# Memory of lines: two multiplications for the next tile, the decay of the state on ScalarE, and tails ahead of the last memory

## The reference, cut to what matters

```python
w1 = (x_prev @ w1w.T).reshape(B, T, H, 4);  w2 = (x @ w2w.T).reshape(B, T, H, 4)
write_lines = exterior(w1, w2)            # 6 differences of products, divided by their norm
r1 = (x @ r1w.T).reshape(B, T, H, 4);       r2 = (x @ r2w.T).reshape(B, T, H, 4)
read_lines = exterior(r1, r2)
Jw = jnp.einsum('bthi,ij->bhtj', write_lines, _J6)
outer = Jw[..., :, None] * Jw[..., None, :]              # 6 x 6 per token and head
# M[t] = sum over s < t of decay ** (t - s) * outer[s]
rd_M = jnp.einsum('bhti,bhtij->bhtj', rd, M_all)
score_M, score_M2 = jnp.sum(rd_M * rd, axis=-1), jnp.sum(rd_M * rd_M, axis=-1)
mem_score = (1 - alpha) * score_M + alpha * score_M2
```

## Time and profile before

| | |
|---|---|
| median of 3 runs | 1919.88 us (1919.46 to 1920.75) |
| the profiled execution | 1922.61 us |
| its span in the profile | 1920.7 us |
| TensorE busy, share of the span | 1856.6 us, 97% |
| VectorE | 1603.5 us, 83% |
| ScalarE | 1491.9 us, 78% |
| GpSimd | 929.2 us, 48% |

### The profile page before, as it was taken

The page is one execution under the profiler, slowest core; times in us unless marked ns, Lnnn a source line. Parts: engine busy times, 40 slices in busy tenths (PEclk is TensorE's granted clock), DMA queues, the critical chain, the costliest instruction groups (busy, mean ns, idle before and its releaser), DMA issues. The chain is left out here.

```text
span 1920.7 us, 61287 instructions
## 1 busy us (share of the span) xinstructions
PE 1856.6 (97%) x22646; PEld 1108.6 (58%) x22646; DVE 1603.5 (83%) x5443; ACT 1491.9 (78%) x4110; POOL 929.2 (48%) x568
## 2 busy tenths in 40 slices
PE   7999999999999989999999999889999999999999
PEld 3777774577775443344444448637777635777754
DVE  5899974899995668999999949979999658999945
ACT  4999995699998362777777763469999847999973
POOL 2788861488883050000000036648888405888820
PEclk9999999999999995999999999999999999999999
DMA  6212230122221041111111000002121201222211
GB/s 179 50 44 50 45 70 6 29 47 48 47 54 42 1 151 38 42 41 41 42 41 41 26 7 5 2 20 51 44 51 44 62 6 36 45 50 45 67 23 44
DMA packets 76330, 85.33 MB, mean 44 GB/s; under 512 B 17327, under 2 KB 50803, under 8 KB 75907
## 3 DMA queue, kind: packets, MB, share of 16 engines
q1 hardware_dynamic: 75839, 81.40, 17.0%
q10 hardware_dynamic: 196, 0.02, 0.0%
HBM read 20.83 MB, written 8.39 MB: 15 GB/s over the span
## 5 line engine op out<-in xcount | busy, mean ns | idle before, releaser
L336 ACT ACTIVATE probs<-probs,negmax 128x128 f32<-128x128 f32 x1024 | 401.9, 402 | 2.3 <-DVE negmax L411 1.9
L2328 ACT ACTIVATE gprobs<-ps_global 128x1024 f32<-128x1024 f32 (+3 forms) x384 | 291.5, 811 | 126.2 <-PE ps_global L1765 103.5
L291 POOL TENSOR_TENSOR rot<-rot 128x1024 f32<-128x1024 f32 x128 | 302.5, 2363 | 143.9 <-DVE rot L381 143.9
L297 POOL TENSOR_TENSOR qk<-rot,cnorm 128x1024 f32<-128x1024 f32 x128 | 244.0, 1906 | 173.6 <-issue 150.9
L304 POOL TENSOR_TENSOR probs<-probs,iden 128x1024 f32<-128x1024 f32 x128 | 243.0, 1898 | 47.2 <-DVE iden L419 46.5
L2010 DVE TENSOR_REDUCE maxes<-ps_global 128x1 f32<-128x512 f32 (+2 forms) x384 | 222.1, 639 | 11.6 <-PE ps_global L1728 6.5
L411 DVE CUSTOM_DVE_ANT_0 probs<-ps_attn,masks 128x128 f32<-128x128 f32 x1024 | 226.2, 287 | 0.8 <-issue 0.8
L336 ACT ACTIVATION_READ_ACCUMULATOR probs<-probs,negmax 128x1 f32 x1024 | 204.2, 199 | 0.0
L1723 PE MATMUL ps_global<-kq 48*128 48x512 bf16 (+3 forms) x768 | 197.3, 346 | 7.1 <-DVE maxes L2010 1.8
L2240 POOL CAST m_parts<-m_turn 32x128 bf16<-32x128 f32 x16 | 4.5, 282 | 364.7 <-DVE m_turn L2024 364.7
L377 DVE TENSOR_TENSOR rot<-ps_attn,rotary 128x512 f32<-128x512 f32 x256 | 175.1, 684 | 1.8 <-PE ps_attn L202 1.5
(11 more groups left out here) (235 smaller groups left out, 4501.5 us busy)
## 6 DMA issues: line engine op xcount, KB each, us to landing
v_first<-v_second SPq DMA_DIRECT2D x256, 128.0 KB, 2.3
hs<-z_a SPq DMA_DIRECT2D x256, 32.0 KB, 1.9
ln<-z_b SPq DMA_DIRECT2D x56, 128.0 KB, 2.4
kq<-split_scratch SPq DMA_DIRECT2D x64, 96.0 KB
kq<-split_scratch SPq DMA_DIRECT2D x64, 64.0 KB
split_scratch<-parts SPq DMA_DIRECT2D x8, 384.0 KB, 4.3
split_scratch<-gprobs SPq DMA_DIRECT2D x6, 384.0 KB, 4.0
x_tok<-in_x_dram SPq DMA_DIRECT2D x4, 512.0 KB, 5.8
```

The costliest lines, as they stand in the source:

```text
L291: nc.gpsimd.tensor_tensor(a, a, b, ALU.add).then_inc(C["rot_sum"], 1)
L297: nc.gpsimd.tensor_tensor(qk[:, k % 2, :].rearrange("p (h d) -> p h d", d=DH), rot_a[:, k % 2, :, :], cnorm[:, k % 2, :].unsqueeze(2).to_b ...
L336: last = nc.scalar.activation(probs[:, k % 2, slot, :], probs[:, k % 2, slot, :], ACT.Exp, scale=-1.0, bias=negmax[:, k % 2, slot:slot + 1 ...
L2328: nc.scalar.activation(probs[:, step % RING, 2 * p:2 * p + 2, 0:w], ps[:, S0 + 2 * p:S0 + 2 * p + 2, 0:w], ACT.Exp).then_inc(C["p2_exp"], 1)
```

## The change

TensorE: `tails` of the next tile comes before the last piece of memory. VectorE: items 0 and 1 of the next turn are multiplied at the end of this turn; the terms, the other multiplications, the reads, the sums of squares, weigh and `advance` get another order; `advance` adds, in two instructions, what ScalarE has scaled. ScalarE: four scalings (`fade`) in each of turns 0 to 5, behind the copy of scores and ahead of left 2; lefts 0 and 1 of the next turn are copied ahead of the two inverses.

```diff
+        faded = sb("faded", [P, GROUPS, B * LINE * LINE])
...
                 lines(4, 6)
-                memories(5, 6)
                 if t + 1 < LAST:
                     tails(t + 1)
+                memories(5, 6)
                 lines(6, 8)
...
                 wait(dve, f"ml_row{(k + 1) % 2}", 16 * ((k + 1) // 2))
+                if k > 0:
+                    wait(dve, "ml_faded", k)
+                    for half in range(2):
+                        at = slice(half * GROUPS // 2, (half + 1) * GROUPS // 2)
+                        last = nc.vector.tensor_tensor(state[:, (k + 1) % 2, at, :].rearrange("p q n -> p (q n)"),
+                                                       faded[:, at, :].rearrange("p q n -> p (q n)"),
+                                                       ps[:, TAIL_BANKS[half], 0:2 * STATE_ROWS], ALU.add)
+                    last.then_inc(C["ml_state"], 1)
+                    return
                 for q in range(GROUPS):
...
-                multiplies(0, 1)
-                all_terms(0, 1)
-                multiplies(1, 2)
-                all_terms(1, 3)
-                multiplies(2, 4)
+                if t == 0:
+                    multiplies(t, 0, 2)
+                all_terms(0, 2)
+                multiplies(t, 2, 3)
+                all_terms(2, 3)
+                multiplies(t, 3, 4)
                 if valid(t):
                     read_memory(t, 0)
                 all_terms(3, 4)
-                multiplies(4, 5)
+                multiplies(t, 4, 5)
                 all_terms(4, 5)
-                multiplies(5, 6)
+                multiplies(t, 5, 6)
                 all_terms(5, 6)
+                multiplies(t, 6, 8)
+                if valid(t):
+                    read_memory(t, 1)
+                multiplies(t + 1, 0, 1)
                 if valid(t + 2):
                     sum_squares(t + 2, 0)
-                if valid(t):
-                    read_memory(t, 1)
-                multiplies(6, 8)
+                multiplies(t + 1, 1, 2)
                 if valid(t):
                     weigh(t)
+                if t + 1 < LAST:
+                    advance(t + 1)
                 if valid(t + 2):
                     sum_squares(t + 2, 1)
-                if t + 1 < LAST:
-                    advance(t + 1)
...
+            def fade(k):
+                wait(act, "ml_state", k)
+                for q in range(GROUPS):
+                    last = nc.scalar.activation(faded[:, q, :], state[:, k % 2, q, :], ACT.Identity, scale=A["whole"][:, q:q + 1])
+                last.then_inc(C["ml_faded"], 1)
...
-                lefts(0, 2)
+                if t == 0:
+                    lefts(t, 0, 2)
                 if valid(t - 2):
                     copy_scores(t - 2)
-                lefts(2, 5)
+                if 0 < t + 1 < LAST:
+                    fade(t + 1)
+                lefts(t, 2, 5)
                 if valid(t):
                     scale_lines(t)
-                lefts(5, 6)
+                lefts(t, 5, 8)
                 if valid(t + 2):
                     square_line(t + 2, 0)
-                lefts(6, 8)
+                lefts(t + 1, 0, 2)
                 if valid(t + 2):
                     inverse(t + 2, 0)
                     square_line(t + 2, 1)
```

More of the change, by code:

```diff
@@ L1560, in global_attention_pass @@
             "ml_outer", "ml_tail", "ml_state", "ml_row0", "ml_row1", "ml_m", "ml_term", "ml_read", "ml_plain", "ml_blend", "ml_weight",
-            "ml_score", "ml_turned", "ml_out"))
+            "ml_score", "ml_turned", "ml_out", "ml_faded"))
     U2 = P2_STEPS
@@ L2124, in body, with multiplies @@
             def body(t):
-                def multiplies(first, end):
+                def multiplies(t, first, end):
                     if valid(t + 2):
@@ L2413, in body, with lefts @@
             def body(t):
-                def lefts(first, end):
+                def lefts(t, first, end):
                     if valid(t + 2):
```

## The result

The median of 8 runs is 1924.94 us (1920.57 to 1927.77) against 1919.67 us in 8 runs of the kernel before (1915.69 to 1920.92): ratio 1.0029, 95% interval 1.0019 to 1.0039. The change costs about 5 us, as forecast (1924.9). The profiled execution took 1924.5 us, its span 1922.6 us, 1.9 longer than before. Its stretch from the first multiplication of turn 0 to the first term of turn 6 is 80.83 us (1150.15 to 1230.98) against 75.93 before (1151.66 to 1227.59), 4.90 longer; the rest of the span is 3.00 shorter, half of it before the stretch, where nothing was changed. So the stretch and its turns are the sharper measure, and they are used from here on. From the start of turn 6 to the first VectorE instruction behind the stage (1242.87 and 1246.26) it is 15.28 us in both.

What follows compares the result with a forecast made beforehand. VectorE was taken to set the 12.31 us turn; new stalls before multiplications 2, 6 and 7 outweigh its savings, making it 13.25. About 5 us more over the stage gives 1924.9 us, range 1918 to 1930 (the forecast's own 1922.5 to 1928).

Steps and rivals of the forecast that it cites:

- The fade ahead of left 2: ScalarE's four fades, 1.27 us, delay left 2, so VectorE stalls 1.5 us before multiplication 2 in turns 1 to 5.
- Multiplications 6 and 7: With tails ahead of the last memory, VectorE stalls 0.55 us before multiplication 6 and 0.39 before 7.
- The other terms of the turn: VectorE's turn: 0.77 us from multiplication 2 to 3, 0.65 from 6 to 7, 4.81 to the next last sum.
- Blend: VectorE's advance: four instructions of 1.10 us become two of 0.74 together, saving 0.36 us a turn.
- The outer product: GpSimd's product is over 3 us into the turn, before tails start on TensorE at 4.4.
- Weigh: Moved later on VectorE, its second instruction no longer waits for GpSimd's subtract: 0.68 us a turn back.
- The tie with the clip: Weigh's second instruction and GpSimd's clip would start nearly together: 0 to 0.25 us a turn, taken as 0.1.
- the rival of GpSimd's outer product in front of weigh: Clip, then normalisation or outer product, come before weigh's second instruction, which waits: +6 to +11, about 1929 us; chance 0.10.
- Start and reciprocal: Turn 1 starts at 1166.69 us against 1165.91; the reciprocal in turn 1 hides in the stall.
- Sum: A full turn takes 13.25 us against 12.31; the stage gets 5.2 us longer.
- a cheap fade: ScalarE's fades only 0.16 us apart: stall 0.9 at multiplication 2, turn 12.6, total +2 us, 1922; chance 0.22.
- VectorE never waiting: The turn shrinks to VectorE's own 10.76 us: 1912 us, or 1917 with TensorE's 0.94 of stalls; chance 0.16.

Runs made afterwards that it cites:

- the fourth experiment: The kernel before with only the fade (ahead of left 2) and the two-instruction blend added, nothing moved: 1920.68 us, ratio 0.9994.
- the first experiment: The changed kernel with the four fades moved in ScalarE's queue from ahead of left 2 to behind left 5: 1924.21 us, ratio 1.0009.
- the best order: Changed kernel, fade behind left 5, second read before multiplication 6, advance behind 7, tails last on TensorE, item 2 ahead of memories: 1917.20 us, ratio 0.9982.
- the third experiment: The changed kernel with tails behind the last memory again on TensorE: 1927.85 us, ratio 1.0029.

## Why the prediction was right

- **The fade ahead of left 2**: left 2 was to start 2.7 us after the last sum of squares and multiplication 2 to start 3.03 after it. It was 2.59 (1191.15 to 1193.74) and 2.92. Four fades were priced at 1.27 us from two rows of other widths; they take 1.23, and doubling them added 1.22 in the turn with a full clock. The Trainium skill (ScalarE: Activation LUTs, "What ACT_TABLE_LOAD costs") has for an activation 186 ns plus 0.833 ns an element, 93 more for a pointer operand, and an overlap of 93 between neighbours: by that, an estimate of 0.31 us from one fade to the next. The trace agrees, with 1.23 over four. Moving the fade alone takes 0.87 us of the 0.99 a turn away.
- **Multiplications 6 and 7**: 0.55 and 0.39 forecast, 0.54 and 0.30 measured. From multiplication 3 to 6 the turn needs 4.13 us (1194.86 to 1198.99), not 3.99: the rest of item 5 until tails takes 0.85 (1195.26 to 1196.11), not 0.69. Tails (1.09) and memory (0.59) are as read from the earlier trace rows. The prediction put this under tails ahead of the last memory; the runs show that the order of those two is worth nothing in the changed kernel. The step beside it is the likelier cause: the read and the sum of squares no longer stand before multiplication 6. No run moves them alone, so this rests on a comparison of kernels that differ in more. With both before it and tails ahead of item 6, as in the kernel before and in the fourth experiment, turns 3 and 4 have no such wait; with neither it is 0.54 to 0.69 us; with the read alone it is 0.39; with the read and with tails behind item 7 it is gone.
- **The other terms of the turn**: 2 to 3 in 0.79 (0.77), 6 to 7 in 0.65, 7 to the last sum of squares in 4.81 (4.81). Together 13.30 against 13.25.
- **Blend**: two instructions that hold VectorE 0.73 us (1203.72 to 1204.45), 0.74 forecast. In the old order its gain was waited away, as the fourth experiment shows.
- **The outer product**: it was to be over 3 us into the turn; it is at 3.59 (1191.17 plus 4.03, the turn starts at 1191.61). Tails start at 4.50, so this cost nothing here, but it is what tails ran into in the first experiment, at 3.63.
- **Weigh**: 0.56 us again, the 0.68 is back. The tie with the clip went VectorE's way by 0.02 us: weigh starts at 1202.66, the clip at 1202.68 takes 0.76 instead of the 0.36 that it takes alone. The 0.1 us a turn set aside for it, 0.6 over the stage, wasn't there, and the rival of GpSimd's outer product in front of weigh did not come.
- **Start and reciprocal**: turn 0 ended as worked out, 0.78 us late. That multiplication 7 comes 9.76 us after the first one in both kernels was taken over and not worked out; the waits on the way are others. The reciprocal stands at the end of turn 1 and takes its 0.46 there; the stall in turn 2 is that much shorter, so it hides, as forecast, one turn later: turn 1 was put at 13.07 and turn 2 at 13.25, together 26.32, and they take 26.43.
- **Sum**: +4.90 us in the stretch where +5.2 was forecast. The 1.9 us by which the profiled execution grew, where 5 was forecast, is this plus 3.0 us elsewhere that go the other way. Of these, 1.12 lie right behind the stage, where TensorE's clock fell in the profiled execution of the kernel before and not in that of the changed one. The same instructions, before and then after:

```profile
1242.87:1252.43 9.56, 7.92 (x33) 2.87 (x33) 6.46 (x11) 2.36 (x4) 6.23 (x5) 0.82 0.00 0
1246.26:1254.70 8.44, 6.69 (x33) 2.24 (x33) 6.27 (x11) 2.36 (x4) 6.18 (x5) 1.00 0.00 0
```

Where the other 1.9 us are stays open. Over 8 runs each the medians differ by 5.3. That the median met the forecast within 0.1 us is luck: the interval is 3.8 us wide, and the errors of the terms cancel (multiplication 2 was 0.11 us a turn earlier, multiplication 6 took 0.14 longer, and the 0.6 us of collision didn't come).
- **The rivals**: a cheap fade (0.16 apart) is out by the 1.23. VectorE never waiting is out for this order; its own work of 10.76 us was a fair target all the same: in the best order the turn is 11.38, of which VectorE is busy 10.96.

## What to carry to other kernels

Work given to an idle engine costs by its place in that engine's queue, not by its share of busy time: ScalarE was busy less than half of the turn, and four activations of 1.23 us cost 0.87 us a turn at one place and nothing that was measured at another. Follow the last thing of a turn (here a sum of squares) through each engine to the first thing of the next that waits for it, and keep everything else behind that. Expect the removal of a stall to be worth less than the stall, since what it covered is late next (1.21 us shorter at one point, 0.87 in the turn), and look for a gain where several waits go at once (12.18 to 11.38 us).

## What the runs showed of the hardware

TensorE's clock fell inside turns that differ little from others at full clock. In the third experiment it stood at a mean of 0.66 from 1220 to 1225 us, so partly at 1.2 GHz, after idle times of 0.96 and 0.73 us; the same two stand in turns 3 and 4 of that kernel, with 1.00:

```profile
1205.07 1.49 PE L1822 MATMUL ps_global<-v_all,decay 128*128 128x144 f32 x10 [0.96 <-DVE kq L2045]
1207.28 0.59 PE L1796 MATMUL ps_global<-wlines_sb,z_a 128*128 128x192 f32 x2 [0.73 <-DVE parts L2031]
...
1218.37 1.49 PE L1822 MATMUL ps_global<-v_all,decay 128*128 128x144 f32 x10 [0.96 <-DVE kq L2045]
1220.58 0.81 PE L1796 MATMUL ps_global<-wlines_sb,z_a 128*128 128x192 f32 x2 [0.73 <-DVE parts L2031]
1221.19 0.84 PE L1798 MATMUL ps_global<-wlines_sb,z_a 128*128 128x192 f32 x2
```

It cost 1.51 us in that turn (14.28 against 12.77). With the doubled fade and an idle time of 1.95 us it was 0.51 over 6.5 us. Of turns 1 to 5 of that kernel the clock was below 1.00 in four and full in turn 2, with idle times of 1.37 and 1.54 us there. Those four turns make up the 8 us by which the stretch is longer than expected (95.2 against 87.0). Behind the stage of the kernel before, after idle times of 1.09 and 0.48 us, it was 0.60 from 1244 to 1248 us; the changed kernel has the same two idle times there and 1.00. So a stall of VectorE that leaves TensorE idle can have a second price which its length doesn't show, and whether it is paid can differ between two turns with the same waits. That it is the idle time which lets the clock fall is not shown by itself, and what decides between such turns these runs don't tell.
